# Gathering x rows into the message buffer and scattering 12 of 40 layer-0 groups inside the layer-norm pass of a two-layer graph network

## The chip, the cores and the metric

One core of one Trainium2 chip. The metric is the device time of one execution in microseconds; lower is better. Engines are named TensorE (PE in the rows), VectorE (DVE), ScalarE (ACT), GpSimd (POOL) and SyncE (SP). A name with a q behind it, as SPq, is the engine's sequencer, which issues DMAs.

## What is computed

There are N = 100,000 nodes with 128 features and E = 25,000 edges (`src`, `dst`), sorted by `dst`. `dst` is drawn so that low node numbers are frequent: the edge at share q of the list has a `dst` of about N q squared. `src` is uniform.

```
h  = relu(layernorm(x))                                   # 100,000 x 128
m  = h[src] + relu(edge_attr @ We + be)                   # 25,000 x 128
a  = (1 + eps) * h + segment_sum(m, dst)
a  = relu(batchnorm(a @ W1 + b1)); a = relu(batchnorm(a @ W2 + b2))
x  = x + a
h  = relu(layernorm(x))
deg = count of each node in src;  norm = deg^-1/2[src] * deg^-1/2[dst]
x  = x + segment_sum(norm * h[dst], src) @ W.T + b
```

## The kernel before

The output tensor in HBM serves as `table`: first it holds h, then h plus the aggregated messages, then x of layer 1, then the result. Between stages all engines meet at a barrier (the end of each `nc.Block()`).

**LN pass.** 50 steps over 49 blocks of 2048 nodes and 50 groups of 512 edges. SP loads a block in two halves into one of four buffers, loads the group's edge features, and stores the block of four steps back from one of two output buffers `hb` (L356). VectorE takes statistics of the block (L387) and of the group's gathered x rows (L390), a chain of small operations gives scale `rs` and shift `nm` (L401 to L422), and it makes the messages: `hs` from the gathered rows (L430), then relu plus edge features into `msgs` (L435). ScalarE normalises the block, 16 activations (L467), and may write an `hb` only when the store of two steps back has landed; it also copies TensorE's results (L474, L480). GpSimd gathers the x rows of the group with four indirect DMAs (L373) into a ring of four buffers `xs`; before that it copies the indices to `gi` (L369), and it waits until the messages of four groups back are made. The pass runs in hardware loops with four steps in the body.

**Dedup stage.** An accumulating scatter must not name a row twice in one DMA, and two of them must not overlap on a row. So the messages go out in NS = 40 groups of G1 = 5 tiles of 128 edges. For a group SP loads its keys to all partitions (L650, two buffers), VectorE compares each tile's keys with those of the tiles up to it (`compare`, L740) and works out where each row goes, its own node or a trash row (`place`, L747, L750). TensorE sums equal keys' messages (`sums`, 15 products, L800), ScalarE writes the sums back (L862), and GpSimd scatters the 5 tiles (L701), after the scatter of the group before has landed; it counts landed groups in `s_landed`. In the same loop VectorE writes one-hots of the `src` keys (`one_hots`, L727, L728) and TensorE counts degrees from them (`counts`, L810). There is one set of five one-hot buffers, so `one_hots(g)` waits until TensorE has used those of g - 1. When all are counted the inverse square roots go to a table in HBM (`dis_ready`).

**Pass 1** (matrix W1). SP loads table blocks of 1024 rows (L668), each when enough groups have landed, and TensorE, ScalarE and VectorE transpose, multiply, keep and take statistics. **Pass 2** (W2 statistics) and **pass 3** (W2, add x, store) follow; a third of the intermediate stays in SBUF, in the same memory as `msgs`. **Layer 1's edge part** shares pass 3's block: GpSimd gathers 200 tiles of rows (L1043), each group of them after the blocks it needs are stored and after the SBUF it fills is free, then scatters 25 groups of 8 tiles (L1056) in the way of layer 0.

**Degree gathers.** GpSimd needs 400 small indirect gathers from the degree table (L564). They are spread: from the group after FILL on, EACH of them go ahead of each scatter group; behind the last scatter they go on up to DEG_1, all in the dedup and pass 1 block; pass 2's block takes DEG_1 to DEG_2; pass 3's block takes the rest, ahead of the row gathers. GpSimd's program for a scatter group is

```
if g > FILL:
    if g == FILL + 1: pool.wait_ge(dis_ready, 16 * HALVES)
    gather_degrees(pool, EACH * (g - FILL - 1), EACH * (g - FILL))
pool.wait_ge(s_pay, g + 1); pool.wait_ge(s_dest, g + 1)
if g: pool.wait_ge(s_sent[(g - 1) % 2], ...); pool.sem_inc(s_landed, 1)
```

The dedup stage and pass 1 are one block, in which each engine's program is an unrolled list.

## Time and profile before

| | us |
|---|---|
| median of 3 runs | 2172.61 (2166.89 to 2173.92) |
| the profiled execution | 2184.82 |
| its span | 2183.1 |

| stage | from, to | PE busy | DVE busy | ACT busy | POOL busy | DMA share |
|---|---|---|---|---|---|---|
| LN pass | 14, 424 | 214.8 | 327.5 | 348.6 | 219.7 | 0.85 |
| dedup stage | 427, 672 | 226.3 | 232.1 | 32.8 | 155.6 | 0.43 |
| pass 1 | 672, 1025 | 282.4 | 132.5 | 195.1 | 259.5 | 0.88 |
| pass 2 | 1025, 1237 | 171.5 | 134.7 | 121.8 | 151.3 | 0.52 |
| pass 3 | 1237, 1629 | 293.1 | 186.2 | 225.9 | 284.0 | 0.95 |
| layer 1's edges | 1629, 1729 | 75.5 | 89.3 | 41.6 | 74.2 | 0.36 |
| and its scatters | 1729, 2183 | 213.0 | 205.4 | 106.8 | 322.7 | 0.38 |

Times are from the span's start. Busy is the time in which an engine ran an instruction; waiting and the issuing of DMAs by SP are not in it. GpSimd is busy while it writes the descriptors of an indirect DMA, and the data move afterwards. The DMA share is the mean busy share of the 16 DMA engines. An engine that is busy for much of a stage need not set its length: what does is read from the waits.

### The profile page before, as it was taken

The numbers are of one execution on the slowest core, as the hardware profiler recorded it, in microseconds if no ns is written. First come the engines' busy times: TensorE is split into PE (matmuls) and PEld (weight loads), VectorE is DVE, ScalarE is ACT, GpSimd is POOL, SyncE is SP. The second block draws the span as 40 slices with busy tenths as digits, with TensorE's granted clock in tenths as the row PEclk, the third lists the DMA queues.
The fourth block names the chain that finished last, engine by engine and source line by source line (L and its number), as shares of the span: only waits on it lengthen the run. The fifth ranks groups of instructions, "written<-read, shape, count | busy, mean of one in ns | idle before, by whom it ended". The sixth has DMA issues, their size and how long they took to land. (4 is left out here: it accounts for less than half of the span.)

```text
span 2183.1 us, 27611 instructions
## 1 busy us (share of the span) xinstructions
PE 1478.3 (68%) x7004; PEld 910.7 (42%) x7004; DVE 1312.0 (60%) x4217; ACT 1073.3 (49%) x1794; POOL 1473.3 (67%) x1274
## 2 busy tenths in 40 slices
PE   3555555399996987786999377767767889880000
PEld 1111111177773544443443134434337888880000
DVE  6888888499993433334777245444459999960000
ACT  4999999411114654564776255555543444430000
POOL 5655555066666678875776777677667777677776
PEclk9999999999998999998999699999987999995555
DMA  6999999344437988897665199999992444433333
GB/s 218 316 311 315 316 329 316 98 86 84 86 68 217 342 231 259 254 289 249 216 206 182 47 368 354 359 363 400 394 338 85 85 71 67 69 42 31 31 29 29
DMA packets 213171, 444.70 MB, mean 204 GB/s; under 512 B 64140, under 2 KB 116502, under 8 KB 206826
## 3 DMA queue, kind: packets, MB, share of 16 engines
q1 hardware_dynamic: 128148, 390.58, 49.6%
q0 software_dynamic: 83200, 52.71, 17.4%
q8 instruction: 44, 0.72, 0.1%
q10 hardware_dynamic: 1728, 0.27, 0.1%
q14 instruction: 51, 0.42, 0.1%
HBM read 279.10 MB, written 164.33 MB: 203 GB/s over the span
## 5 line engine op out<-in xcount | busy, mean ns | idle before, releaser
L701 POOL DMA_INDIRECT out_dram<-big,s_dest_ x200 | 322.2, 1611 | 144.7 <-issue 62.5
L1056 POOL DMA_INDIRECT out_dram<-big,t_dest_ x200 | 322.7, 1613 | 130.0 <-DMA out_dram<-big,t_dest_ 70.9
L1219 PE MATMUL psum<-work,w 128*128 128x512 f32 x392 | 204.2, 646 | 135.0 <-ACT work L1168 135.0
L1043 POOL DMA_INDIRECT big<-out_dram,dst_i x200 | 210.3, 1051 | 77.1 <-issue 65.0
L564 POOL DMA_INDIRECT norm<-inv_sqrt_degree,dst_i x200 | 200.9, 1005 | 79.5 <-issue 74.8
L373 POOL DMA_INDIRECT g_x<-in_x_dram,g_i x200 | 190.4, 952 | 88.2 <-issue 47.5
L467 ACT ACTIVATE big<-n_x,n_nm,n_rs 128x128 f32<-128x128 f32 x592 | 231.5, 481 | 25.5 <-DMA out_dram<-big 25.1
L564 POOL DMA_INDIRECT norm<-inv_sqrt_degree,src_i x200 | 191.3, 957 | 71.5 <-issue 59.7
L510 PE MATMUL psum<-WeB,g_eaT 128*128 128x512 f32 x100 | 103.7, 1141 | 168.2 <-ACT g_eaT L474 168.2
L1067 DVE TENSOR_SCALAR work<-work,cols 128x1024 f32<-128x1024 f32 x98 | 74.6, 761 | 236.8 <-ACT work L1176 236.8
L842 PE MATMUL psum<-work,w 128*128 128x512 f32 x392 | 197.0, 628 | 0.0
L522 DVE BATCH_NORM_STATS2 stat<-work 128x6 f32<-128x512 f32 (+1 forms) x138 | 84.9, 659 | 146.3 <-ACT work L858 146.3
L1168 ACT ACTIVATE work<-work,bn_t,bn_s 128x1024 f32<-128x1024 f32 x66 | 81.7, 1240 | 184.0 <-DMA work<-y_feature_major 151.8
L923 PE MATMUL psum<-work,w 128*128 128x512 f32 x392 | 170.9, 599 | 0.0
L818 PE MATMUL psum<-ident,rows 128*128 128x128 f32 x784 | 111.0, 288 | 68.5 <-DMA rows<-out_dram 68.2
L1219 PEld LDWEIGHTS psum<-work,w 128*128 128x128 f32 x392 | 70.8, 201 | 201.1 <-ACT work L1168 119.0
L522 DVE BATCH_NORM_STATS2 stat<-psum 128x512 f32 (+2 forms) x202 | 127.0, 672 | 44.5 <-PE psum L923 44.5
L818 PEld LDWEIGHTS psum<-ident,rows 128*128 128x128 f32 x784 | 94.7, 148 | 134.2 <-DMA rows<-out_dram 89.7
L800 PE MATMUL psum<-big,work 128*128 128x128 f32 x1200 | 144.2, 279 | 6.2 <-DVE work L740 6.1
L800 PEld LDWEIGHTS psum<-big,work 128*128 128x128 f32 x1200 | 139.5, 193 | 17.9 <-DVE work L740 16.1
L862 ACT ACTIVATE big<-psum,sign 128x640 f32<-128x640 f32 x40 | 31.8, 794 | 218.4 <-PE psum L800 218.4
L870 ACT ACTIVATE work<-psum 128x1024 f32<-128x1024 f32 x98 | 100.1, 1021 | 76.5 <-PE psum L818 76.3
(157 smaller groups left out, 3104.3 us busy)
## 6 DMA issues: line engine op xcount, KB each, us to landing
work<-y_feature_major SPq DMA_DIRECT2D x132, 512.0 KB, 6.1
rows<-out_dram SPq DMA_DIRECT2D x98, 512.0 KB, 5.8
rows<-in_x_dram SPq DMA_DIRECT2D x98, 512.0 KB, 6.6
out_dram<-rows SPq DMA_DIRECT2D x97, 512.0 KB, 6.0
out_dram<-big SPq DMA_DIRECT2D x48, 1024.0 KB, 7.5
n_x<-in_x_dram SPq DMA_DIRECT2D x74, 512.0 KB, 5.8
y_feature_major<-work SPq DMA_DIRECT2D x66, 512.0 KB, 5.5
rows<-in_dst_dram SPq DMA_DIRECT2D x39, 320.0 KB, 3.4
```

The costliest lines, as they stand in the source:

```text
L373: pool.indirect_dma_start(out=xs[u][:, j, :], out_offset=None, in_=x[:, :], in_offset=bass.IndirectOffsetOnAxis(ap=gi[u][:, j:j + 1], axis ...
L467: a = act.activation(hb[u % 2][:, c, :], xb[u][:, c, :], ACT.Relu, bias=nm[u][:, c:c + 1], scale=rs[u][:, c:c + 1])
L522: m = dve.bn_stats(kept(stat, n), part)
L564: pool.indirect_dma_start(out=flat(norm[n])[:, t:t + 1], out_offset=None, in_=dis_tab[:, :], in_offset=bass.IndirectOffsetOnAxis(ap=flat(e ...
L701: pool.indirect_dma_start(out=table[:, :], out_offset=bass.IndirectOffsetOnAxis(ap=dest[:, t:t + 1], axis=0), in_=flat(msgs)[:, t * D:(t + ...
L800: m = nc.tensor.matmul(tot_p[g % 2][:, o * D:(o + 1) * D], pairs(g % SAME, j, o, o + 1), flat(msgs)[:, t * D:(t + 1) * D], start=(j == o), ...
L818: m = nc.tensor.transpose(psum[k % 2][:, c * P:(c + 1) * P], rows[k % B][:, c, :], ident[:, :])
L842: m = nc.tensor.matmul(psum[2 + k % 2][:, h * BANK:(h + 1) * BANK], w1[:, :], feats[k % 2][:, h * BANK:(h + 1) * BANK], start=True, stop=True)
L923: m = nc.tensor.matmul(psum[u % 3][:, h * BANK:(h + 1) * BANK], w2[:, :], feats[u % 2][:, h * BANK:(h + 1) * BANK], start=True, stop=True)
L1043: pool.indirect_dma_start(out=msgs[:, g, j * D:(j + 1) * D], out_offset=None, in_=out[:, :], in_offset=bass.IndirectOffsetOnAxis(ap=dst_i[ ...
L1056: pool.indirect_dma_start(out=out[:, :], out_offset=bass.IndirectOffsetOnAxis(ap=dest[:, g * G2 + j:g * G2 + j + 1], axis=0), in_=flat(msg ...
L1219: m = nc.tensor.matmul(psum[u % 2][:, h * BANK:(h + 1) * BANK], w2[:, :], feats[u % 2][:, h * BANK:(h + 1) * BANK], start=True, stop=True)
```

## The change

**Gathers.** GpSimd gathers x rows straight into `msgs`, group after group, with the indices `src_i` itself; `xs`, `gi` and the wait for the messages go. It waits for the gather of two groups back. VectorE reads and overwrites the same tile.

**Twelve groups early.** The LN pass is unrolled. `scatter`, `compare`, `place`, `sums` and `keep` become shared functions. At the steps k = 10, 13, ..., 43 (`early_at`) VectorE compares and places one group behind the messages of that step, TensorE sums it two steps later in `psum[3]` (the edge-feature ring shrinks from four banks to three), and ScalarE keeps it. The key loads stand in SP's queue ahead of a store. GpSimd scatters the twelve groups behind all fifty gather groups, each when the table blocks that it needs have been stored (`n_landed`, `need_0`, worked out by `blocks_needed`).

**The dedup stage** takes groups 12 to 39. The degree counts of all 40 are spread over these 28 (`counted`: one or two each).

**Degree gathers.** FILL 19 to 23, EACH 4 to 5, DEG_1 96 to 170, DEG_2 256 to 330.

The diff, cut to its core (the moved functions are unchanged in what they do):

```diff
-    FILL = 19
-    EACH = 4
-    DEG_1 = 96
-    DEG_2 = 256
+    EARLY, FIRST_AT, SPACING = 12, 10, 3
+    FILL = 23
+    EACH = 5
+    DEG_1 = 170
+    DEG_2 = 330
...
     @block.sync (LN pass)
+        g = early_at(k + 2)
+        if g is not None:
+            wait(sp, s_same, G1 * (g - 1))
+            sp.dma_start(keyT_e[g % 2][:, :], dst[G1 * P * g:G1 * P * (g + 1)].rearrange(
+                "(a e) -> a e", a=1).broadcast_to((P, G1 * P))).then_inc(s_kin[g % 2], 16)
+        if has_block(k - RN):
+            store(k - RN)
...
     @block.gpsimd (LN pass)
-        def gather(i, u):
-            g = RN * i + u
-            wait(pool, g_h, g - RN + 1)
-            pool.sem_inc(pool_go, 1)
-            pool.tensor_copy(gi[u][:, :], kept(src_i, g)).then_inc(g_gi, 1)
-            wait(pool, g_gi, g + 1)
+        for g in range(NG):
+            wait(pool, g_xs[g % 2], 16 * J * (g // 2))
             pool.sem_inc(pool_go, 1)
             for j in range(J):
                 pool.indirect_dma_start(
-                    out=xs[u][:, j, :], out_offset=None, in_=x[:, :],
-                    in_offset=bass.IndirectOffsetOnAxis(ap=gi[u][:, j:j + 1], axis=0)).then_inc(g_xs[u], 16)
+                    out=msgs[:, g, j * D:(j + 1) * D], out_offset=None, in_=x[:, :],
+                    in_offset=bass.IndirectOffsetOnAxis(ap=src_i[:, g, j:j + 1], axis=0)).then_inc(g_xs[g % 2], 16)
+        pool.wait_ge(e_row, 3)
+        for g in range(EARLY):
+            pool.wait_ge(n_landed, pool.value_load(need_0[0:1, g:g + 1], min_val=1, max_val=NBIG))
+            scatter(pool, g)
...
     @block.vector (LN pass)
             messages(k)
+            blocks_needed(k)
+            g = early_at(k)
+            if g is not None:
+                dve.wait_ge(g_msg, k + 1)
+                compare(dve, g, same_e, keyT_e)
+                place(dve, g)
...
     @block.scalar (LN pass)
+            g = early_at(k - 2)
+            if g is not None:
+                keep(act, g, psum[3])
...
     @block.tensor (LN pass)
+            g = early_at(k - 2)
+            if g is not None:
+                sums(pe, g, same_e, psum[3], 1)
...
+            def counted(g):
+
+                done = (g - EARLY) * NS // (NS - EARLY)
+                return range(done, (g + 1 - EARLY) * NS // (NS - EARLY))
...
     @block.vector (dedup stage)
-                    for g in range(NS):
-                        compare(g)
-                        place(g)
-                        one_hots(g)
+                    for g in range(EARLY, NS):
+                        compare(dve, g, same, keyT)
+                        place(dve, g)
+                        for n in counted(g):
+                            one_hots(n)
...
     @block.tensor (dedup stage)
-                    for g in range(NS):
-                        sums(g)
-                        counts(g)
+                    for g in range(EARLY, NS):
+                        sums(pe, g, same, tot_p[g % 2], 2)
+                        for n in counted(g):
+                            counts(n)
```

## Rows read from the trace of the kernel before

**Rows 1.** Stretches: busy us by engine, clock, DMA share, GB/s.

```profile
120.00:200.00 80.00, 43.40 (x51) 12.28 (x50) 68.59 (x343) 73.32 (x198) 46.30 (x53) 1.00 0.93 316
...
1237.00:1629.00 392.00, 293.10 (x1176) 161.13 (x1176) 186.20 (x199) 225.85 (x196) 284.00 (x278) 0.95 0.95 358
```

**Rows 2.** Timeline of ScalarE, LN pass: start, us, instruction, idle before.

```profile
202.30 6.26 ACT L467 ACTIVATE big<-n_x,n_nm,n_rs 128x128 f32<-128x128 f32 x16 [0.94 <-DMA out_dram<-big]
...
209.30 6.25 ACT L467 ACTIVATE big<-big,n_nm,n_rs 128x128 f32<-128x128 f32 x16
...
217.61 6.26 ACT L467 ACTIVATE big<-n_x,n_nm,n_rs 128x128 f32<-128x128 f32 x16 [1.23 <-DMA out_dram<-big]
```

**Rows 3.** Timeline of VectorE and SP in the same steps.

```profile
204.68 0.69 DVE L435 SCALAR_TENSOR_TENSOR big<-g_hs,g_ef 128x512 f32 x1 [0.16 <-DVE g_hs L430]
...
210.12 0.36 SPq L356 DMA_DIRECT2D out_dram<-big  x1
...
211.40 0.69 DVE L435 SCALAR_TENSOR_TENSOR big<-g_hs,g_ef 128x512 f32 x1 [0.16 <-DVE g_hs L430]
```

**Rows 4.** DMA queues and issues of the LN pass, 120 to 360 us.

```profile
q0 software_dynamic: 4016, 8.22, 12.3%
...
g_x<-in_x_dram,g_i POOLq DMA_INDIRECT x126, 4.9
```

**Rows 5.** One group's timeline in the dedup stage; all its compares by line.

```profile
522.47 3.51 PE L800 MATMUL psum<-big,work 128*128 128x128 f32 x30
522.68 0.28 DVE L727 TENSOR_SCALAR rows<-rows 128x256 f16<-128x256 f16 x1
...
524.98 0.34 DVE L740 SCALAR_TENSOR_TENSOR work<-rows,dst_k,upto 128x128 f32<-128x128 int32 x1
...
525.82 2.32 PE L810 MATMUL psum<-rows 128*128 128x512 f16 x10
...
L740 DVE SCALAR_TENSOR_TENSOR work<-rows,dst_k,upto 128x128 f32<-128x128 int32 (+4 forms) x200 | 110.8, 610 | 2.7 <-DMA rows<-in_dst_dram 2.7
```

**Rows 6.** Timeline of SP and GpSimd at both ends of pass 1.

```profile
672.16 4.17 SPq L668 DMA_DIRECT2D rows<-out_dram  x5
...
679.51 1.55 POOL L701 DMA_INDIRECT out_dram<-big,s_dest_  x1 [5.66 <-DMA out_dram<-big,s_dest_]
...
1018.07 0.95 POOL L564 DMA_INDIRECT norm<-inv_sqrt_degree,src_i  x1 [0.30 <-issue]
1025.73 0.94 POOL L564 DMA_INDIRECT norm<-inv_sqrt_degree,src_i  x1 [6.70 <-POOLq L644]
```

**Rows 7.** Groups of GpSimd in pass 1: count, busy, mean ns, idle.

```profile
L701 POOL DMA_INDIRECT out_dram<-big,s_dest_ x106 | 166.6, 1572 | 54.1 <-issue 34.5 <-DMA out_dram<-big,s_dest_ 19.5
L564 POOL DMA_INDIRECT norm<-inv_sqrt_degree,src_i x96 | 92.9, 968 | 33.4 <-issue 28.3 <-DMA out_dram<-big,s_dest_ 5.1
```

**Rows 8.** Groups of GpSimd's instructions, pass 3 to 1729 us.

```profile
L1043 POOL DMA_INDIRECT big<-out_dram,dst_i x200 | 210.3, 1051 | 77.1 <-issue 65.0 <-DMA big<-out_dram,dst_i 10.4 <-ACT work L1168 1.2
L564 POOL DMA_INDIRECT norm<-inv_sqrt_degree,dst_i x144 | 148.0, 1027 | 55.3 <-issue 50.5 <-POOLq L883 4.8
```

**Rows 9.** Timeline, layer 1: first group kept, first scatter.

```profile
1668.12 1.02 ACT L1195 ACTIVATE big<-psum 128x1024 f32<-128x1024 f32 x1 [6.52 <-PE psum L1250]
...
1729.11 2.47 POOL L1056 DMA_INDIRECT out_dram<-big,t_dest_  x1 [5.77 <-issue]
```

**Rows 10.** GpSimd's gathers of x in the LN pass.

```profile
L373 POOL DMA_INDIRECT g_x<-in_x_dram,g_i x200 | 190.4, 952 | 88.2 <-issue 47.5 <-POOL g_i L369 40.7
```

**Rows 11.** DMA queues and issues of pass 1, 690 to 770 us.

```profile
q0 software_dynamic: 4091, 1.58, 18.3%
...
out_dram<-big,s_dest_ POOLq DMA_INDIRECT x25, 6.1
```

**Rows 12.** GpSimd's scatters in the dedup stage.

```profile
L701 POOL DMA_INDIRECT out_dram<-big,s_dest_ x94 | 155.6, 1655 | 90.7 <-DMA out_dram<-big,s_dest_ 35.0 <-issue 27.9 <-ACT big L862 24.3
```

**Rows 13.** SP's loads of pass 1 up to 770 us: first and last start.

```profile
L668 SPq DMA_DIRECT2D rows<-out_dram x36: 327/328/715, 672.2 to 769.0; - x36
```

More of the change, by code:

```diff
@@ new lines, in preln_gin_then_gcn, with scatter @@
+        dest = sb("s_dest_", [P, NTILE], i32, place_scope)
+        NS = NTILE // G1
+        LASTS = E // (P * G1)
+        PAIRS = G1 * (G1 + 1) // 2
+        assert NS * G1 == NTILE and LASTS == NS - 1 and NS <= P and NB <= P and EARLY < LASTS
+        def scatter(pool, g):
+            pool.wait_ge(s_pay, g + 1)
+            pool.wait_ge(s_dest, g + 1)
+            if g:
+                pool.wait_ge(s_sent[(g - 1) % 2], 16 * G1 * ((g - 1) // 2 + 1))
+                pool.sem_inc(s_landed, 1)
+            pool.sem_inc(pool_go, 1)
+            for j in range(G1):
+                t = g * G1 + j
+                pool.indirect_dma_start(
+                    out=table[:, :], out_offset=bass.IndirectOffsetOnAxis(ap=dest[:, t:t + 1], axis=0),
+                    in_=flat(msgs)[:, t * D:(t + 1) * D], in_offset=None, compute_op=ALU.add).then_inc(s_sent[g % 2], 16)
@@ new lines, in compare @@
+        def compare(dve, g, same, keyT):
+            dve.wait_ge(s_kin[g % 2], 16 * (g // 2 + 1))
+            wait(dve, s_tot, g - len(same) + 1)
+            if g == LASTS:
+                dve.memset(keyT[g % 2][:, E - g * G1 * P:G1 * P], PAD).then_inc(s_pad, 1)
+                dve.wait_ge(s_pad, 1)
+            for j in range(G1):
+                t = g * G1 + j
+                dve.scalar_tensor_tensor(out=pairs(same[g % len(same)], j, 0, j + 1), in0=keyT[g % 2][:, 0:(j + 1) * P],
+                                         scalar=flat(dst_k)[:, t:t + 1], in1=upto[:, (G2 - 1 - j) * P:G2 * P],
+                                         op0=ALU.is_equal, op1=ALU.mult, accum_out=seen[:, t:t + 1]).then_inc(s_same, 1)
@@ new lines, in place, with sums @@
+        def place(dve, g):
+            dve.wait_ge(s_same, G1 * (g + 1))
+            dve.scalar_tensor_tensor(out=tiles(hop, g), in0=tiles(seen, g), scalar=1.0, in1=tiles(gap, g),
+                                     op0=ALU.not_equal, op1=ALU.mult).then_inc(s_hop, 1)
+            dve.wait_ge(s_hop, g + 1)
+            dve.tensor_tensor(tiles(dest, g), tiles(hop, g), tiles(flat(dst_k), g), ALU.add).then_inc(s_dest, 1)
+        def sums(pe, g, same, tot, depth):
+            pe.wait_ge(s_same, G1 * (g + 1))
+            wait(pe, s_pay, g - depth + 1)
+            for o in range(G1):
+                for j in range(o, G1):
+                    t = g * G1 + j
+                    m = nc.tensor.matmul(tot[:, o * D:(o + 1) * D], pairs(same[g % len(same)], j, o, o + 1),
+                                         flat(msgs)[:, t * D:(t + 1) * D], start=(j == o), stop=(j == G1 - 1))
+            m.then_inc(s_tot, 1)
@@ L348, in edge_features @@
                                 "(j p) d -> p j d", p=P)).then_inc(g_ea[u], 16)
[L349 removed]
+                            if g == GFULL:
                                 sp.dma_start(ea[u][0:TREST, n, :], edge_attr[TFULL * P:E, :]).then_inc(g_ea[u], 16)
[L352 to L356 removed]
@@ L357, in _, with store @@
-                        steps(sp, NG, RN, load, RN)
+                        def store(k):
+                            sp.wait_ge(n_h, 2 * (k + 1))
+                            lo = SEEN_BIG if k == NBIG - 1 else 0
+                            sp.dma_start(big_rows(table, k, lo), hb[k % 2][lo:P].rearrange("p c d -> p (c d)")).then_inc(n_out[k % RN], 16)
+                        for k in range(NG):
+                            load(k)
                         for k in range(NG - RN, NBIG):
-                            store(k // RN, k % RN)
+                            store(k)
@@ L498, in _ @@
+                        landed(NBIG - 2)
+                        landed(NBIG - 1)
                     @block.tensor
                     def _(pe):
[L500 to L510 removed]
```

348 lines of the change are left out of this document (162 added, 186 removed).

## The prediction

> **What bounds the kernel now.** I read the page's slices first, then the busy time by stage, then inside each stage the timeline around whatever waits. There are six stages: the LN pass (14 to 424 us), the dedup stage of layer 0 (427 to 658, with its degree tail to 672), pass 1 (672 to 1025), pass 2 (1025 to 1237), pass 3 (1237 to 1629), and the edge part of layer 1 with its scatters (1629 to 2183). No engine bounds all of them [rows 1].
>
> The LN pass is held by a loop through two output buffers. An apply that starts at 202.30 takes 6.26 us, its store is issued at 210.12, and the next apply on that buffer starts at 217.61, released by that store: 6.26 + 1.56 + 7.49 = 15.3 us for two steps, 7.65 a step, where ScalarE alone would need 7.0 (202.30 to 209.30) [rows 2, 3]. The store's landing is long because the DMA engines are 0.93 busy [rows 1, 4]. VectorE does a step in 6.7 us (204.68 to 211.40) and finishes a step's messages about 3.5 us before ScalarE ends that step's apply [rows 2, 3].
>
> In the dedup stage TensorE and VectorE share the bound: the group sums take 3.5 us and the group's degree counts 2.3 on TensorE; one-hots 2.3 (522.68 to 524.98) and compares 2.8 (110.8 us over 40 groups), with some 0.4 of placing, on VectorE. 230 us over 40 groups is 5.75 a group [rows 5]. GpSimd scatters meanwhile, and is only at group 19 when the degree table is ready and pass 1 begins to load, at 672.16 [rows 6]. From there GpSimd is the chain: 20 more groups with 4 degree gathers before each, 16 gathers behind them, the last at 1018, and the barrier opens at 1025 [rows 6, 7]. The last blocks of pass 1 wait for the last scatter, so its arithmetic ends no sooner. Pass 2 has 160 degree gathers at 1.25 us, 200 us of its 212. In pass 3 GpSimd does 144 degree gathers and then the 200 row gathers of layer 1, which run 100 us past the end of pass 3; so the layer-1 scatters start at 1729.11, although the first group's sums were kept at 1669.1 [rows 8, 9]. They then run to the end, 18.2 us a group, and ask for nothing but GpSimd.
>
> So what counts is GpSimd's chain from 672 on, and before it the time at which that chain can start.
>
> **The parts of the change, with costs.**
>
> (1) *Gathers straight into the message buffer.* The wait for the messages of four groups back and the small index copy go, and with them 41 us in which the gathers stood behind that copy [rows 10]. GpSimd was not late in the LN pass, so this is worth nothing by itself. It now runs ahead: four gathers at 0.95 + 0.30 are 5.0 us a group, if the group two back has landed. Landing is 4.9 us at present [rows 4, 10]. With the DMA engines fuller I take 5.3, so 50 groups end at 14.5 + 265 = 280 us. Bounds: 5.0 (264) and, with landings of 7 us, 5.75 (302).
>
> (2) *Twelve groups within the LN pass.* VectorE gets 3.3 us more in each third step, 3 x 6.7 + 3.3 = 23.4 us per three steps, 7.8 a step. That is 0.15 above the present 7.65 over the 34 steps between first and last group, 5 us. It starts 3.5 us ahead, so the key load that SP queues before a store finds its buffer free about when SP comes to it. TensorE gets 3.5 us of sums every third step and is busy 43 us of 80, so it has over 3 us free in each; ScalarE gets a copy of 0.8 us every third step and has 0.6 us of waiting in each [rows 1, 2]. Both are covered. The DMA engines get 60 scatters and 12 key loads of 320 KB. A scatter cost about 0.57 us of all 16 engines in pass 1 (18.3% of 80 us for 25 of them, the small gathers between them taken off) [rows 11]; a key load, by its bytes at the LN pass's 316 GB/s, 1.0: 34 + 12 = 46 us, on a pass of 410 us that has some 24 us free at its present share. That makes 20 to 25 us more for the store loop.
>
> GpSimd itself: its scatters can start only after all 50 gather groups, at 280. A group is 5 x (1.66 + 0.30) = 9.8 us, plus the wait for its last landing, 2.4 us when landings take 3.4, and 2.7 more when they take 6.1 as in pass 1 [rows 11, 12]. That is 14.9 a group; 12 groups, less the last wait, 174 us: GpSimd is done at 454 and the barrier opens at 455 or so. Before it opened at 424. So GpSimd ends the LN pass, not the stores (446): **+31 us**. Bounds: landings of 3.4 and gathers at 5.0 put GpSimd at 406, and the stores with half the extra DMA time at 436, +12; gathers at 5.75 and scatters at 16.3 (pass 1's cadence without its gathers) put GpSimd at 490, +66.
>
> The Trainium skill ("SBUF — State Buffer", the box on VectorE blocking DMA) says that GpSimd cannot write its descriptors while VectorE runs an fp32 operation in its two-port mode. The rows show far less: a scatter instruction took 1655 ns while VectorE was busy throughout and 1572 ns in pass 1 [rows 7, 12]. By the rows it is 5 us over 60 scatters, already in the 1.66; by the page, if the 2.8 us of compares of each group stopped GpSimd whole, it would be 34 us more. That is a rival below.
>
> (3) *The dedup stage with 28 groups, but still 40 groups of degree counts.* The counts are spread: 16 groups carry one, 12 carry two. There is one set of one-hot buffers, and a set is rewritten only when TensorE has used the previous one. With two, VectorE writes the first set (2.3), then must wait until TensorE has done the group's sums and the first counts (3.4 + 2.2 after the compares), writes the second (2.3) and only then compares the next group (2.8), for which TensorE waits in turn. So a group with two counts costs 5.5 + 2.3 + 2.8 = 10.6 us and not 5.75 + 2.3 [rows 5]. 16 x 5.75 + 12 x 10.7 = 220 instead of 230, and the tail of 14 us is the same: I take **-8 us**. Bound on the other side: without that stall VectorE's own work sets it, 28 x 6.7 = 188, -42.
>
> (4) *GpSimd around pass 1.* At 12.2 us a group it scatters 12 to 23 within 157 us of the stage's start and then stands before group 24, because the degree gathers wait for the table, some 237 us after the start: 24 groups are done then, before it was 20. From the table on: 16 groups of 5 x (0.97 + 0.30) + 5 x (1.57 + 0.30) = 15.7 us. The landing waits were 19.5 us for 20 groups behind four gathers each, 1 us a group [rows 7]; behind five gathers, 1.25 us more of cover, I take 0.5: 16.2 x 16 = 259. Then 4.5 for the last landing, 90 gathers at 1.25, 112, and 6 of barrier: 382 us. Before, from 672.2 to 1025.1, 353. **+29 us.** Pass 1's own work covers none of it: its loads came at (769.0 - 672.2) / 35 = 2.8 us a block while they had no scatter to wait for [rows 13], which is 98 x 2.8 + 15, about 290 us. Bounds: no landing wait, +21; 0.9 us a group, +36.
>
> (5) *Pass 2* has 160 degree gathers as before: 0.
>
> (6) *Pass 3 and after.* 70 degree gathers instead of 144, at (148.0 + 55.3 - 4.8) / 144 = 1.38 us each [rows 8]: the row gathers start 97 us into the pass, not 199. At 1.44 us [rows 8] they need 288, but the last groups need the last blocks of pass 3 stored, about 400 us into it; they end at 418. The first kept group is there at 432 (1669.1 - 1237). So the scatters start at 432 instead of 492: -60. Against it: some 58 row gathers more fall into pass 3, whose DMA engines are 0.95 busy, at 0.23 us each (12.3% of 240 us for 126) [rows 1, 4], 13 us at most, 8 taken; and three groups more of scatters run beside a busy VectorE, 24 at the 0.1 us above and some landings, 4. **-48 us.** Bounds: -60 and -38.
>
> **Sum** against the profiled execution, 2184.8 us (span 2183.1): 31 - 8 + 0 + 29 - 48 = +4. Its share of the median, 2172.6, is 0.9944; +4 us there is 2177.
>
> **The rivals.**
>
> *The LN pass has room for it* (ends on the other side). Landings stay at 3.4 to 5 us, GpSimd is done at 406 to 420, the stores set the end at 436. For it: the pass is only 0.93 busy, and unrolling spares SP the register arithmetic between its DMAs. Against: pass 1's share of 1.0 brought landings of 6.1. +12 instead of +31: -15 us, 2158. It decides if GpSimd's first scatter group takes under 13 us.
>
> *GpSimd is much later in the LN pass.* Gathers that keep rushing fill the queue, land in 7 us, and the scatters follow at 16.3: +66 instead of +31, +39 in all, 2211. For it: the scatters' rate is pass 1's. Against: the store loop lets the DMA engines rest as soon as it is late.
>
> *The one-hot wait isn't paid,* -42 instead of -8: -30 us, 2143. Against: the buffers are one set in the code, and TensorE's program order is fixed.
>
> *VectorE locks GpSimd out,* 34 us more in the LN pass, +38 in all, 2210. [...] Against: the difference of 0.08 us in [rows 7, 12].
>
> **How the numbers follow.** Forecast 0.43 (its own range, from -13 to +23 us, is 2160 to 2195), room in the LN pass 0.27, GpSimd much later 0.17, no one-hot wait 0.07, lock-out 0.03, something else 0.03. 2177 is the likeliest's time. The range: the bounds and all but the ends of the two outer cases, -32 to +42 us, 2141 to 2214. A measurement of this kernel tells 0.3%, 6.5 us. Of the forecast's 0.43 a fifth is faster than that, two fifths the same, two fifths slower. Faster: 0.09 + 0.22 + 0.07 + 0.01 = 0.39. Same: 0.17 + 0.05 = 0.22. Slower: 0.17 + 0.17 + 0.03 + 0.02 = 0.39.
>
> **What would show it.** LN pass: first scatter near 280 us, one group each 15 us, barrier near 455 with GpSimd last. Dedup stage: 220 us, groups of 5.7 and 10.7 us, TensorE idle some 3 us before the sums that follow a double count. GpSimd idle about 80 us before group 24. Pass 1 about 380 us with GpSimd alone for its last 80 or so. Layer-1 scatters starting right at the first kept group, 432 us after pass 3 starts. The prediction is wrong if the LN pass ends before 440 or after 480, or if the dedup stage takes under 200 us.

## The result, and the profile after

The changed kernel takes 2215.8 us in the median of 4 runs (2206.0 to 2224.7), beside 2173.3 us (2166.9 to 2177.8) for the kernel before on the same chip: ratio 1.019, interval 1.015 to 1.023. It is 43 us slower where +4 was forecast, and 2 us outside the range. The profiled execution has a span of 2223.0 us against 2183.1, so the trace holds 39.9 us of it.

Timeline of the kernel after (start, us, instruction, idle before it and what ended it): GpSimd at the end of the LN pass.

```profile
296.69 0.99 POOL L464 DMA_INDIRECT big<-in_x_dram,src_i  x1 [0.30 <-issue]
297.99 1.62 POOL L183 DMA_INDIRECT out_dram<-big,s_dest_  x1 [0.30 <-issue]
...
314.67 1.97 POOL L183 DMA_INDIRECT out_dram<-big,s_dest_  x1 [7.51 <-DMA out_dram<-big,s_dest_]
...
453.49 1.55 POOL L183 DMA_INDIRECT out_dram<-big,s_dest_  x1 [2.77 <-DMA out_dram<-big,s_dest_]
465.10 1.55 POOL L183 DMA_INDIRECT out_dram<-big,s_dest_  x1 [2.62 <-DMA out_dram<-big,s_dest_]
479.49 0.56 POOL L795 IOTA rows<- 128x512 int32 x1 [5.40 <-POOLq L416]
```

The gathers of x end at 297 us and not at 280. Each L183 row is the start of a scatter group: 17 us apart at first, beside the pass's loads and stores, of which some 7.6 us are the wait for the last landing (16.3 on the average of the seven groups to 412 us), and 11.6 apart at the end, with a wait of 2.7. The barrier opens at 479.5 (before: 424.1). VectorE has nothing to do for the last 58 us, as its row shows. SP issues the last store at 419.9 and waits 18.4 us for it (second row: engine and line, waited for, us in total, times, longest), so the stores are done at some 438.5, and the 41 us from there to the barrier are GpSimd's alone:

```profile
479.50 0.36 DVE L835 TENSOR_REDUCE work<-dst_k 128x40 f32<-128x200 f32 x1 [58.35 <-PEq L416]
...
SPq L416 <- DMA out_dram<-big: 18.4, 1, 18.4
```

The gathers of x and the scatters of the LN pass by group (count, busy us, mean ns, idle before and its causes); below, SP's stores issued from 120 to 297 us (count, KB, us to landing; before, from 120 to 360 us: 7.5), and the stretch 200 to 290 us (busy us by engine, clock, DMA share, GB/s).

```profile
L464 POOL DMA_INDIRECT big<-in_x_dram,src_i x200 | 197.6, 988 | 88.3 <-issue 62.8 <-DMA big<-in_x_dram,src_i 25.5
L183 POOL DMA_INDIRECT out_dram<-big,s_dest_ x60 | 95.1, 1584 | 81.3 <-DMA out_dram<-big,s_dest_ 49.2 <-issue 14.9 <-DVE s_dest_ L224 9.3
...
out_dram<-big SPq DMA_DIRECT2D x22, 1024.0 KB, 8.2
...
200.00:290.00 90.00, 52.42 (x151) 28.62 (x152) 83.74 (x409) 81.59 (x216) 63.85 (x64) 0.62 0.95 326
```

GpSimd stood 25.5 us for landings of its own gathers: (298.0 - 13.6) / 50 is 5.7 us a group, not 5.3.

The dedup stage: a group with two counts and its successor, TensorE's timeline; then two short stretches, in which the granted clock is the third number from the end, behind the five busy times.

```profile
557.73 3.62 PE L233 MATMUL psum<-big,work 128*128 128x128 f32 x30
561.18 2.32 PE L879 MATMUL psum<-rows 128*128 128x512 f16 x10
564.14 2.44 PE L879 MATMUL psum<-rows 128*128 128x512 f16 x10 [0.65 <-DVE rows L833]
568.67 5.24 PE L233 MATMUL psum<-big,work 128*128 128x128 f32 x30 [2.09 <-DVE work L214]
...
570.00:573.80 3.80, 3.80 (x22) 3.79 (x21) 3.80 (x16) 0.00 (x0) 3.19 (x3) 0.55 0.66 104
573.80:576.00 2.20, 2.20 (x12) 1.11 (x11) 0.91 (x4) 0.79 (x1) 1.69 (x2) 1.00 0.55 96
```

The double takes 10.9 us from sums to sums; TensorE stands idle 2.1 us before the next group's sums, and these take 5.24 us instead of 3.51: in the 3.8 us from 570.0 on its granted clock is near the lower of its two levels (0.55; 0.5 is 1.2 GHz, 1.00 is 2.4 GHz). Pass 1 and the rest, GpSimd and SP:

```profile
729.00 0.80 SPq L769 DMA_DIRECT2D inv_sqrt_degree<-rows  x2
732.51 4.04 SPq L783 DMA_DIRECT2D rows<-out_dram  x5
...
993.88 1.55 POOL L183 DMA_INDIRECT out_dram<-big,s_dest_  x1 [0.30 <-issue]
1003.32 1.02 POOL L689 DMA_INDIRECT norm<-inv_sqrt_degree,src_i  x1 [7.88 <-DMA out_dram<-big,s_dest_]
...
1114.91 0.95 POOL L689 DMA_INDIRECT norm<-inv_sqrt_degree,src_i  x1 [0.30 <-issue]
1125.37 0.95 POOL L689 DMA_INDIRECT norm<-inv_sqrt_degree,src_i  x1 [9.52 <-POOLq L759]
...
1334.29 0.95 POOL L689 DMA_INDIRECT norm<-inv_sqrt_degree,dst_i  x1 [4.77 <-POOLq L950]
...
1740.71 0.94 POOL L1108 DMA_INDIRECT big<-out_dram,dst_i  x1 [0.30 <-issue]
1765.87 1.71 POOL L1121 DMA_INDIRECT out_dram<-big,s_dest_  x1 [24.21 <-issue]
...
1763.90 1.03 ACT L1260 ACTIVATE big<-psum 128x1024 f32<-128x1024 f32 x1 [6.60 <-PE psum L1315]
```

They answer to [rows 6, 9]. After the last scatter (993.9) come 110 us of degree gathers and nothing else: in pass 2's first rows ScalarE and VectorE have waited 100 us. The layer-1 scatters now start on the first kept group (1763.90 + 1.03), no longer on the last row gather.

Stage by stage, in us, from the profiled executions. The first load of pass 1 stands for the table.

| Stage | Before | After | Change | Forecast |
|---|---|---|---|---|
| LN pass, to its barrier | 424.1 | 479.5 | +55 | +31 |
| Barrier to the table (dedup stage) | 248.1 | 253.0 | +5 | -8 |
| Pass 1 | 353.6 | 392.9 | +39 | +29 |
| Pass 2 | 211.7 | 208.9 | -3 | 0 |
| Pass 3 to the first layer-1 scatter | 491.6 | 431.6 | -60 | -60 + 8 |
| Layer-1 scatters to the end | 454.0 | 457.1 | +3 | +4 |
| Sum | | | +40 | +4 |

### The profile page after: what moved, and what is told of

Its sections match the earlier page's. It is cut to its first block and busy times, and to the rows that moved or that the text cites. A ratio compares the mean times of both kernels' runs of the same rounds, so it can differ in the third digit from the quotient of the medians.

```text
span 2223.0 us, 26530 instructions
## 1 busy us (share of the span) xinstructions
PE 1458.1 (66%) x7006; PEld 921.0 (41%) x7006; DVE 1313.1 (59%) x4222; ACT 1073.0 (48%) x1794; POOL 1442.2 (65%) x1224
## 5 line engine op out<-in xcount | busy, mean ns | idle before, releaser
L183 POOL DMA_INDIRECT out_dram<-big,s_dest_ x200 | 319.4, 1597 | 175.7 <-DMA out_dram<-big,s_dest_ 90.9
L1121 POOL DMA_INDIRECT out_dram<-big,s_dest_ x200 | 329.6, 1648 | 144.7 <-issue 80.4
L1284 PE MATMUL psum<-work,w 128*128 128x512 f32 x392 | 202.5, 641 | 129.2 <-ACT work L1233 129.1
L1108 POOL DMA_INDIRECT big<-out_dram,dst_i x200 | 204.1, 1021 | 111.5 <-issue 80.4
L464 POOL DMA_INDIRECT big<-in_x_dram,src_i x200 | 197.6, 988 | 88.3 <-issue 62.8
L689 POOL DMA_INDIRECT norm<-inv_sqrt_degree,dst_i x200 | 194.0, 970 | 69.4 <-issue 64.7
L622 PE MATMUL psum<-WeB,g_eaT 128*128 128x512 f32 x100 | 92.3, 1022 | 146.1 <-ACT g_eaT L585 145.9
L912 PE MATMUL psum<-work,w 128*128 128x512 f32 x392 | 186.0, 598 | 0.0
L990 PE MATMUL psum<-work,w 128*128 128x512 f32 x392 | 170.8, 598 | 0.4 <-ACT work L979 0.4
L1233 ACT ACTIVATE work<-work,bn_t,bn_s 128x1024 f32<-128x1024 f32 x66 | 81.7, 1239 | 181.5 <-DMA work<-y_feature_major 152.5
L979 ACT ACTIVATE work<-work,bn_t,bn_s 128x1024 f32<-128x1024 f32 x66 | 81.7, 1240 | 129.2 <-PEq L759 100.2
L233 PE MATMUL psum<-big,work 128*128 128x128 f32 x840 | 112.5, 298 | 29.3 <-DVE work L214 29.3
L887 PE MATMUL psum<-ident,rows 128*128 128x128 f32 x784 | 105.5, 278 | 32.4 <-DMA rows<-out_dram 32.4
L233 PEld LDWEIGHTS psum<-big,work 128*128 128x128 f32 x840 | 109.1, 212 | 38.3 <-DVE work L214 36.9
```

Of the source, the lines that this page charges most:

```text
L183: pool.indirect_dma_start(out=table[:, :], out_offset=bass.IndirectOffsetOnAxis(ap=dest[:, t:t + 1], axis=0), in_=flat(msgs)[:, t * D:(t + ...
L233: m = nc.tensor.matmul(tot[:, o * D:(o + 1) * D], pairs(same[g % len(same)], j, o, o + 1), flat(msgs)[:, t * D:(t + 1) * D], start=(j == o ...
L464: pool.indirect_dma_start(out=msgs[:, g, j * D:(j + 1) * D], out_offset=None, in_=x[:, :], in_offset=bass.IndirectOffsetOnAxis(ap=src_i[:, ...
L689: pool.indirect_dma_start(out=flat(norm[n])[:, t:t + 1], out_offset=None, in_=dis_tab[:, :], in_offset=bass.IndirectOffsetOnAxis(ap=flat(e ...
L887: m = nc.tensor.transpose(psum[k % 2][:, c * P:(c + 1) * P], rows[k % B][:, c, :], ident[:, :])
L912: m = nc.tensor.matmul(psum[2 + k % 2][:, h * BANK:(h + 1) * BANK], w1[:, :], feats[k % 2][:, h * BANK:(h + 1) * BANK], start=True, stop=True)
```

## The experiments

Each is an edit of the changed kernel. The stages are read as above, from GpSimd's timeline of the profiled execution; its time is up to 9 us off the median of its kernel (changed: 2224.7 against 2215.8). The ratio is the measure of a kernel as a whole: beside the experiments the kernel before took 2179 us in the median, and 2173 beside the changed one, so that a difference between the medians of an experiment and of the changed kernel is uncertain by some 6 us. "Dedup and pass 1" runs from the LN barrier to the start of pass 2, and "pass 3" to the first layer-1 scatter. The ratio is to the kernel before. Four kernels with the same LN pass (the changed one, e1, e2, e5) opened that barrier at 479, 474, 472 and 479, so a difference of some 7 us in that stage is not to be explained.

| Kernel | LN | Dedup and pass 1 | Pass 2 | Pass 3 | Rest | Median | Ratio (interval) |
|---|---|---|---|---|---|---|---|
| before | 424 | 602 | 212 | 492 | 454 | 2173.3 | 1 |
| changed | 479 | 646 | 209 | 432 | 457 | 2215.8 | 1.019 (1.015 to 1.023) |
| e1_degrees | 474 | 545 | 211 | 483 | 452 | 2168.1 | 0.995 (0.993 to 0.998) |
| e2_fill31 | 472 | 563 | 209 | 434 | 457 | 2138.4 | 0.983 (0.978 to 0.987) |
| e3_early8 | 433 | 633 | 209 | 431 | 457 | 2166.8 | 0.995 (0.993 to 0.997) |
| e4_mixed | 458 | 636 | 209 | 436 | 451 | 2192.4 | 1.007 (1.005 to 1.009) |
| e5_two_sets | 479 | 600 | 209 | 437 | 457 | 2175.3 | 0.998 (0.995 to 1.000) |
| e6_direct | 428 | 589 | 211 | 487 | 456 | 2173.3 | 0.997 (0.995 to 0.999) |
| e7_all | 439 | 545 | 209 | 439 | 461 | 2092.4 | 0.960 (0.957 to 0.964) |
| e8_mixed22 | 439 | 634 | 209 | 434 | 452 | 2174.4 | 0.999 (0.996 to 1.001) |
| e9_ring3 | 459 | 643 | 209 | 435 | 457 | 2201.5 | 1.010 (1.007 to 1.013) |
| e10_split | 437 | 509 | 196 | 463 | 458 | 2064.0 | 0.948 (0.945 to 0.951) |
| e11_split140 | 437 | 503 | 186 | 480 | 455 | 2066.4 | 0.950 (0.947 to 0.953) |

**e1_degrees: the split of the degree gathers as before.**

```diff
-    DEG_1 = 170
-    DEG_2 = 330
+    DEG_1 = 96
+    DEG_2 = 256
```

> The changed kernel, but with the split of the degree gathers as it was before: 96 of the 400 by the end of pass 1 (not 170) and 160 in pass 2, so 144 in pass 3. Theory A (in pass 1 GpSimd alone sets the time, in pass 3 it does not as long as its row gathers end before the first sums of layer 1 are kept): from the table on GpSimd needs 271 us for its 16 groups, 16 more gathers (20 us) and the 9.5 us at the barrier, 301 us in place of 393, unless the pass's own loads and matmuls need some 290 to 300, which bounds it at about the same figure; so -92 there. In pass 3 the row gathers start 74 gathers later and run past the end of the pass: the layer-1 scatters start 492 us after pass 3's start and not 432, +60. In all -32 us against the changed kernel's 2223 us span, about 2184 in the median. Theory B (pass 1 also waits for something else, its loads or stores beside the scatters, so that fewer gathers do not shorten it): pass 1 stays above 340 us, the end is +10 to +60, over 2225.

Pass 1 fell by 100 us (293 from GpSimd's first degree gather, in place of 393), and the layer-1 scatters came 483 us after the start of pass 3, 51 later than in the changed kernel. The median fell by 48 us. That is theory A's mechanism, with a better price at both ends than it named (-92 and +60). The 74 gathers that were moved forward cost 100 us of pass 1 and buy 51 of pass 3. With 293 us pass 1 is also where the expectation had its loads and matmuls as a bound (290 to 300), so this run does not tell which of the two ends it.

```profile
1706.92 1.71 POOL L1108 DMA_INDIRECT big<-out_dram,dst_i  x1 [0.31 <-issue]
1712.49 1.61 POOL L1121 DMA_INDIRECT out_dram<-big,s_dest_  x1 [3.86 <-issue]
...
1658.35 1.02 ACT L1260 ACTIVATE big<-psum 128x1024 f32<-128x1024 f32 x1 [6.91 <-PE psum L1315]
```

Here the first group was kept at 1659.4, and the scatters waited 53 us for the row gathers, as before the change [rows 9].

**e2_fill31: GpSimd scatters on while the table is not there.**

```diff
-    FILL = 23
+    FILL = 31
```

> The changed kernel, but GpSimd scatters 20 groups (12 to 31) before it waits for the degree table, not 12 (12 to 23), so 8 groups and not 16 are left for pass 1. Theory A (the 94 us in which GpSimd stood before the table were free for scatters): 20 groups at 11.7 us are 234 us, just before the table; pass 1 then has 8 groups of 5 gathers and 5 scatters, 16.2 us each, 130 gathers behind them (163 us) and some 14 us of landing and barrier, 307 us in place of 393; the table comes when it did, 252 us after the barrier. In all -86 us, about 2130 in the median. Theory B (scatters beside the dedup stage hold VectorE or TensorE up, or the loads of pass 1 become the bound at well over 310 us): the stage to the table becomes longer than 258 us, or pass 1 stays over 340 us; -40 or less, over 2175.

Theory A: from the barrier to pass 2 it takes 563 us in place of 646 (-82; -86 expected), and the median fell by 77. SP's first pass-1 load comes 253.2 us after the barrier (725.55 - 472.32), as in the changed kernel, so eight more groups of scatters beside the dedup stage do not delay the table. The rows are this kernel's: the barrier, and the table.

```profile
472.32 0.56 POOL L795 IOTA rows<- 128x512 int32 x1 [5.40 <-POOLq L416]
...
725.55 4.04 SPq L783 DMA_DIRECT2D rows<-out_dram  x5
```

**e3_early8: eight early groups and not twelve.**

```diff
-    EARLY, FIRST_AT, SPACING = 12, 10, 3
+    EARLY, FIRST_AT, SPACING = 8, 10, 3
```

> The changed kernel with 8 groups scattered in the LN pass in place of 12. Theory A (from the end of its gathers, near 297 us, GpSimd alone ends the LN pass, at 17 us a group while the pass's loads and stores run): 8 groups end near 432, the barrier opens between 428 and 436 in place of 479, -43 to -51 us. The dedup stage has 32 groups, 8 of them with a double count; a double costs 11.1 (plus 1.7 at the lower TensorE clock in half of them), a single 5.6: 24 x 5.6 + 8 x 12 = 230, -3. GpSimd has 16 groups before the table (188 us, still done before it), and the rest is the same. In all -45 to -50, about 2168 in the median. Theory B (the stores or VectorE end the LN pass soon after, since the scatters delay them too): the barrier opens over 450, less than -30 us.

```profile
433.04 0.55 POOL L795 IOTA rows<- 128x512 int32 x1 [21.39 <-POOLq L416]
```

The barrier opened at 433, in the range of theory A, with GpSimd waiting 21 us for it: with eight groups GpSimd no longer ends the pass. SP issues its last store there at 415 and waits 17.4 us for it. So the last four groups cost the LN pass 46 us, 11.6 each. In the dedup stage they cost nothing: GpSimd's idle time before the table shrank from 94 to 36 us. The median fell by 49.

**e4_mixed and e8_mixed22: scatters among the gathers.** The two differ in the number (16 or 22); e8 also puts the last two groups behind the last gather.

```diff
-    pool.wait_ge(e_row, 3)
-    for g in range(EARLY):
-        pool.wait_ge(n_landed, ...)
-        scatter(pool, g)
+        e, rest = divmod(g - 16, SPACING)      # in the loop over the gather groups g; e8: 22
+        if rest == 0 and 0 <= e < EARLY:
+            if e == 0:
+                pool.wait_ge(e_row, 3)
+            pool.wait_ge(n_landed, ...)
+            scatter(pool, e)
```

> The changed kernel with the 12 early scatter groups issued among the gathers (one behind every third gather group, from the 17th on) and not behind all of them. Theory A (the cost in the LN pass is GpSimd's order: it stands 7.7 us for each landing with nothing else to issue, after 297 us): the landings are covered by the three gather groups between, GpSimd's work is 50 x 5.3 + 12 x 9.8 = 383 us and it is done before 425; the barrier opens at 425 to 440 in place of 479, -40 to -54 us, about 2168 in the median. The rest is the same. Theory B (the cost is the DMA engines' or the landings' own, whatever the order): scatters among the gathers make the gathers late for VectorE, the steps of the LN pass get longer than 8.3 us and the barrier opens over 460, less than -20 us.

> As the run with the scatters among the gathers, but the first scatter group comes behind the 23rd gather group and not the 17th, and the last two behind the last gather. Theory A (the run before lost its gain because GpSimd stood 40 us for a group's sums to be kept, and so came late with the next gathers, for which VectorE then stood 44 us): with six gather groups more of lead GpSimd waits for no sums and VectorE for no gathers, or under 10 us each; the barrier opens at 430 to 442 us in place of 479 (458 with the smaller lead), -38 to -50 us against the changed kernel, about 2170 in the median. Theory B (scatters among the gathers and the stores lengthen the steps through the DMA engines): the barrier stays over 450.

With 16 it was neither theory: barrier at 458, -21, between the two ranges. GpSimd's scatters in the LN pass, and VectorE's wait for x rows, in e4:

```profile
L183 POOL DMA_INDIRECT out_dram<-big,s_dest_ x65 | 107.7, 1657 | 59.0 <-ACT big L240 39.8 <-issue 18.6 <-DMA big<-in_x_dram,src_i 0.6
...
L486 DVE BATCH_NORM_STATS2 n_st<-big x200: 263/275/296, 20.5 to 429.6; 128x6 f32<-128x128 f32 x100
its engine sat idle before it (us, times) until:
  DMA big<-in_x_dram,src_i: 44.0, 14
```

GpSimd waited 39.8 us for sums to be kept (11.5 of them at the start of the dedup stage) and not once for a scatter's landing; then it came late with the gathers, and VectorE stood 44 us for them. The landings were covered, as theory A says, and VectorE stood for gathers, as theory B says, but for another reason than B's: early group e is placed in step 10 + 3e and summed two steps later, and GpSimd's queue has the wait for these sums ahead of gathers that the next steps need. With six groups more of lead (e8) VectorE waited 5.6 us and the barrier opened at 439, with GpSimd 28 us early for it:

```profile
L489 DVE BATCH_NORM_STATS2 n_st<-big x200: 263/275/295, 20.3 to 403.3; 128x6 f32<-128x128 f32 x100
its engine sat idle before it (us, times) until:
  DMA big<-in_x_dram,src_i: 5.6, 2
...
439.12 0.55 POOL L800 IOTA rows<- 128x512 int32 x1 [28.14 <-POOLq L416]
```

So all twelve groups fit into the LN pass at 11.5 us over a pass with one (428, e6), and 15 over the kernel before. In the changed kernel it was the order, and not the DMA engines, that cost the 40 us more.

**e5_two_sets: a second set of one-hot buffers.**

```diff
-            wait(dve, a_used, G1 * g)
+            wait(dve, a_used, G1 * (g - 1))
 ...
-    dve.tensor_scalar(hot_r[j], ...
+    dve.tensor_scalar(hot_r[g % 2][j], ...      # the same for hot_c and in counts
```

> The changed kernel with two sets of one-hot buffers in the dedup stage, used in turn; nothing else differs. Theory A (a group with two counts is long because the second set has to wait for the first, and the sums after it run at the lower TensorE clock because TensorE stood idle): a double costs VectorE 2.8 + 0.4 + 4.6 = 7.8 us and TensorE 3.5 + 4.4 = 7.9 in place of 11, the sums stay at 3.5 us, so 16 x 5.6 + 12 x 7.9 = 184 us in place of 233; from the barrier to the table 205 us in place of 252.7, GpSimd stands some 47 us before the table in place of 94, and the rest is the same: -45 to -48 us, some 2170 in the median. Theory B (the engines' own work or the landing of the key loads sets these groups): -10 or less.

TensorE's timeline in this kernel, a group with two counts and the sums of the next; then GpSimd's first degree gather:

```profile
571.94 3.51 PE L233 MATMUL psum<-big,work 128*128 128x128 f32 x30
575.29 2.32 PE L879 MATMUL psum<-rows 128*128 128x512 f16 x10
577.45 2.32 PE L879 MATMUL psum<-work 128*128 128x512 f16 x10
579.84 3.62 PE L233 MATMUL psum<-big,work 128*128 128x128 f32 x30
...
...
686.25 1.03 POOL L689 DMA_INDIRECT norm<-inv_sqrt_degree,src_i  x1 [39.31 <-DMA inv_sqrt_degree<-rows]
```

A double takes 7.9 us, as expected to the tenth, the sums behind it 3.6, and GpSimd reaches the table 207.6 us after the barrier (478.7) and not 252.6: -45. The median fell by 41.

**e6_direct: the first part of the change nearly alone.**

```diff
-    EARLY = 12, FILL = 23, EACH = 5, DEG_1 = 170, DEG_2 = 330
+    EARLY =  1, FILL = 19, EACH = 4, DEG_1 =  96, DEG_2 = 256
```

> The first part of the change nearly alone: x rows gathered straight into the message buffer and the LN pass unrolled, but only 1 group scattered early, and the split of the degree gathers and the order of the dedup stage's scatters as before (19 and 4, 96 and 256). Theory A (gathers that run ahead are worth nothing and cost nothing, since the store loop sets the LN pass): barrier at 420 to 430 us, the rest as before, within 6 us of the kernel before, ratio 0.997 to 1.003. Theory B (gathers that rush crowd the DMA engines and the store loop, or SP's and GpSimd's savings shorten it): barrier outside 415 to 435, ratio off by over 0.5%.

Theory A at its edge: ratio 0.997 (0.995 to 0.999), barrier at 427.6. The gathers end at 293 us here too, and behind one scatter group GpSimd stands 125 us. The LN pass is no shorter than before (428 and 424), so gathers that run ahead are worth nothing by themselves. The 13 us less between barrier and pass 2 (589, not 602) go with the one group that was taken out of that stretch: GpSimd comes to its first degree gather 252 us after the barrier and not 265.

**e9_ring3: three groups of x rows in flight and not two.**

```diff
-    g_xs = sems("g_xs", 2)
+    g_xs = sems("g_xs", 3)
 ...
-    wait(pool, g_xs[g % 2], 16 * J * (g // 2))
+    wait(pool, g_xs[g % 3], 16 * J * (g // 3))      # the same in then_inc and in VectorE's wait
```

> The changed kernel, but a group of x rows may be gathered when the group three back has landed, not two back (three semaphores in turn). Theory A (the first scatter came at 298 us and not at 280 because GpSimd stood 25 us for landings of its own gathers, and whatever it saves there comes off the end of the LN pass): gathers at 5.05 us a group end at 266 to 270 us, the scatters follow from there at 15 to 17 us a group, the barrier opens at 450 to 458 us in place of 479, -21 to -29 us. Theory B (the gathers go as fast as the DMA engines take them, or faster ones make the stores and the scatters' landings later by as much): first scatter after 285, or the scatter groups at over 17 us, barrier over 468, -10 us or less.

```profile
274.31 1.96 POOL L183 DMA_INDIRECT out_dram<-big,s_dest_  x1 [0.31 <-issue]
...
459.12 0.55 POOL L795 IOTA rows<- 128x512 int32 x1 [5.56 <-POOLq L416]
```

The scatters start at 274 and not at 298, and the barrier opens at 459 and not at 479: of 24 us, 20 arrive, just short of theory A's range and far from B's. GpSimd waited 4.9 us for landings of gathers and not 25.5. So the two-deep wait of the gathers was a price of the LN pass. The groups are still 15.5 us apart while the pass loads and stores (274.3 to 413.6, nine of them).

**e7_all, e10_split, e11_split140: the repairs together.** All three have e8's order, e5's two sets and `FILL = 28`; they differ in where the degree gathers go:

```diff
-    DEG_1 = 170,  DEG_2 = 330
+    DEG_1 = 150,  DEG_2 = 310      # e7_all
+    DEG_1 = 120,  DEG_2 = 270      # e10_split
+    DEG_1 = 120,  DEG_2 = 260      # e11_split140
```

> All repairs together: scatters of 12 groups among the gathers from the 23rd on, two sets of one-hots, GpSimd scattering to group 28 before the table, 150 degree gathers by the end of pass 1 and 310 by the end of pass 2. Theory A (the four costs found are separate and from the barrier to the end of pass 1 only GpSimd's own work is left): barrier 435; from there 28 groups x 11.9 + 150 x 1.26 + some 20 of start, landing waits and barrier = 540 less what the gathers hide of landings, 525; pass 2 209, pass 3 to the first layer-1 scatter 433, the scatters 456: 2058, some 2060 in the median, ratio to the kernel before 0.944. Theory B (the repairs compete for the same cover, above all pass 1's own loads and matmuls, 290 to 300 us from the table at 205): not under 2100.

> The run with all repairs, with 120 degree gathers by the end of pass 1 (not 150) and 270 by the end of pass 2 (not 310), 130 in pass 3. Theory A (passes 1 and 2 are set by GpSimd's gathers at 1.25 us each, and pass 3 pays for what is left to it only as far as its row gathers run past the first kept sums): pass 1 -37 (under 280 us from its first degree gather, or held at some 270 to 280 by its own loads), pass 2 with 150 gathers -12, the layer-1 scatters 463 us after pass 3's start in place of 439, +24; -25 us against 2092, 2067 in the median. Theory B (pass 2's matmuls set it at 209 whatever the gathers, or pass 1 its loads at over 295): -10 or less, over 2080.

> As the run before in this call, but only 140 gathers in pass 2, so 140 in pass 3. Theory A (pass 2 is GpSimd's alone down to there): pass 2 -25 against 209, 184 us; layer-1 scatters 477 us after pass 3's start, +38; -25 against 2092. Theory B (pass 2 has a floor of its own between 190 and 205 us, from TensorE's 171 us and its loads): pass 2 no shorter than with 150 gathers, so 10 to 14 us slower than the run with 150.

e7 gave 2092: under theory B's 2100, but 32 over the 2060 of A. Most of it is 20 us between barrier and pass 2 (545, not 525). Of GpSimd's 17 groups there before its first degree gather, each took 13 us and not 11.9:

```profile
L183 POOL DMA_INDIRECT out_dram<-big,s_dest_ x85 | 143.8, 1692 | 87.0 <-ACT big L240 36.9 <-issue 25.2 <-DMA out_dram<-big,s_dest_ 24.9
```

GpSimd waits there for sums to be kept too (36.9 us, some 12 of them at the stage's start), and an instruction takes 1692 ns. The repairs are thus not wholly separate. How much of the 13 us is the wait for sums and how much the longer instruction, no run tells. e10 and e11 behave as theory A: pass 2 with 150 gathers takes 196 us and with 140 it takes 186, so it is GpSimd's alone down to there; pass 3 pays 24 and 41 us for what is left to it; 2064 and 2066 in the median, 5% under the kernel before. e10 is the fastest version of this study. Between it and e11 the split is flat. How much of the 5% needs the early groups is not shown: no run has the kernel before with its gathers split and its scatters ordered anew and no group early.

## Why the prediction was wrong

Against the forecast of +4 the trace holds +40. The LN pass, the dedup stage and pass 1 came out 24, 13 and 10 us above their terms, and passes 2 and 3 and the end together 12 us below theirs.

**(1)** *Gathers end at 280* was mis-sized: 297. The step took 5.3 us a group and had 5.75 as a bound; it was 5.7. That a group waits for the landing of the group two back was in the working; the 25.5 us that it would cost were not. e9 priced it: -20 us for a third group in flight.

**(2)** *+31 in the LN pass* is the step that failed most: +55, half a microsecond inside the 480 from which the prediction would have called itself wrong. Its mechanism is right (GpSimd, not the stores, ends the pass), and its size is off at both terms: the start is 18 us late, and from the first scatter to the barrier it takes 479.5 - 298.0 = 181.5 us where 455 - 280 = 175 were forecast. While the pass loads and stores, a group waits some 7.6 us for its landing, where 5.1 were allowed; for the last groups, with the stores done, it is 2.7, which hides most of that error in the sum. What happened is the second rival, "GpSimd much later", at +55 of its +66. "Stores end at 446" was too late: they are done at some 438.5, and e8, where GpSimd stands 28 us early, opens at 439. That is 14 to 15 us over the kernel before and not 22. Whether these are DMA time is open, for VectorE is busy 282 of the 300 us from 100 to 400 (before: 253).

What the forecast did not look for is the order. Behind the gathers GpSimd has nothing else in its queue while a group lands, and each landing costs it the whole wait. e8 gives the same scatters and gathers to the same engine, and takes 40 us less.

**(3)** *-8 in the dedup stage* was mis-sized: +5. The stall itself came as forecast: doubles of 11.0 us on the average of 11 (10.7 forecast). Missing was TensorE's clock. The sums behind six of the 11 stalls took 5.2 us and not 3.5, which made those groups 7.2 us and not 5.65 (9.5 us in all); behind the other five, which stood idle as long (2.1 us), they took at most 3.6, and why is open. The rest are the doubles' own 0.3 us (3 in all) and the stage's first group, 8.6 us where it was 7.3 before. The Trainium skill ("TensorE: Matmul & The Clock Gate", HAM oscillation) describes a TensorE that waits for loads between short bursts, falls back to the lower clock in each wait and starts each burst at it. The trace agrees in kind: 0.55 at 570.0 to 573.8 us behind a TensorE idle for 2.1 us, 1.00 just after, and in e5, without the stall, at most 3.6 us for the sums of every group but the first. e5 shows that stall and clock were worth 45 us together (table at 208 us after the barrier and not 253). Against the kernel before (248) that is -40, where -42 was the bound for a stage without the stall.

**(4)** *+29 in pass 1* was mis-sized: +39. The reading holds in each part: GpSimd stood 94 us before group 24, and then set the pass alone. 16 groups took 263 us (16.5 each, 16.2 forecast), the last landing 7.9 and not 4.5, the 90 gathers 113, the barrier 9.5 and not 6. That 94 idle us could be used here (e2), and that gathers cost more here than they give back (e1), could have been read from the prediction's own numbers (80 us idle; 74 gathers at 1.25 us are 92, for 60 in pass 3), and it did not ask.

**(5)** and **(6)** held: pass 2 -3, the first layer-1 scatter at 431.6 us (432), on the first kept group. Of the +8 for row gathers in pass 3 nothing showed; of the +4 behind, 3 us did.

**The rivals.** *Room in the LN pass*: refuted, its point of decision was a first group under 13 us, and it took 17. *One-hot wait not paid*: refuted in the changed kernel, made true in e5. *VectorE locks GpSimd out*: refuted in size for these compares. A scatter instruction took 1555 ns on the average beside an idle VectorE and 1599 in the LN pass, under 3 us over the 60 early scatters, not 34; the gathers of x, beside which eight of the twelve groups were compared, took 988 ns, and 986 in e6 with one group. It took most in e7's dedup stage, 1736 ns from 450 to 590 us, where VectorE is busy 138.5 of 140 us with compares and one-hots. That is 12% more, and no run shows whether VectorE is the cause. The first row is the changed kernel's from 422 us on, the second its 298 to 421, the third and the stretch e7's 450 to 590.

```profile
L183 POOL DMA_INDIRECT out_dram<-big,s_dest_ x20 | 31.1, 1555 | 21.8 <-DMA out_dram<-big,s_dest_ 16.9 <-issue 4.9
...
L183 POOL DMA_INDIRECT out_dram<-big,s_dest_ x40 | 64.0, 1599 | 59.6 <-DMA out_dram<-big,s_dest_ 32.3 <-issue 10.1 <-DVE s_dest_ L224 9.3
...
L183 POOL DMA_INDIRECT out_dram<-big,s_dest_ x52 | 90.3, 1736 | 58.4 <-ACT big L240 33.1 <-DMA out_dram<-big,s_dest_ 12.8 <-issue 12.5
...
450.00:590.00 140.00, 138.50 (x927) 99.01 (x926) 138.47 (x552) 16.66 (x21) 90.28 (x52) 1.00 0.43 72
```

So the change as a whole: 60 us won in pass 3, given back in three places. The LN pass pays for groups that the dedup stage could have scattered in time that GpSimd then idled; e2 and e3 are two ways to put that right, and each alone beats the kernel before (by 1.7% and 0.5%). Even the 60 us were bought too dear, as e1 shows. What stays open: why a group took 13 us in e7, and the 7 us by which the LN pass differs between kernels in which it is the same.

## What to carry to other kernels

Work moved forward to an engine's idle time is only free if that engine can do it in the order in which its queue has it: put the moved instructions between others that cover their landings, with enough lead that their wait never stands ahead of what the next steps need (e4 and e8 differ in little but that lead, by 19 us). When the balance between two engines changes, read where the freed engine now stands idle, and move the next constants (how many groups before the table, how many gathers in which pass) with it; here the change without this was a loss, and with the order of the queue and a second set of buffers it became a gain of 5%. A stall of TensorE can cost more than its length: behind six of 11 the clock had fallen, and the next sums took 1.6 us longer.

## What the runs showed of the hardware

The recorded clock has to be held against a matmul's own time. In the LN pass before, the record has a granted clock of 1.00 [rows 1], but there two of the pass's matmuls with 512 columns take 2.07 us, just what they take in e6 from 240 to 300 us, where the record says 0.50. In the changed kernel, where it says 0.62, a pair behind a group's sums takes 1.12 us and another 2.07. So by these durations TensorE ran at its lower level in the LN pass before, whatever the record says. The other engines waited 1.0 us for TensorE from 200 to 290 us of the changed kernel, so its clock cost next to nothing there. In the dedup stage record and durations agree (0.55 with 5.24 us, 1.00 with 3.5). The first row is of the kernel before, the next two of e6, the last two of the changed kernel.

```profile
196.42 2.07 PE L508 MATMUL psum<-beB,ones 1*128 1x512 f32 x2
...
242.53 2.07 PE L622 MATMUL psum<-WeB,g_eaT 128*128 128x512 f32 x2 [4.03 <-ACT g_eaT L585]
240.00:300.00 60.00, 32.77 (x39) 9.81 (x40) 51.58 (x253) 52.77 (x143) 43.55 (x42) 0.50 0.97 306
...
221.03 1.12 PE L622 MATMUL psum<-WeB,g_eaT 128*128 128x512 f32 x2
229.25 2.07 PE L622 MATMUL psum<-WeB,g_eaT 128*128 128x512 f32 x2 [5.93 <-ACT g_eaT L585]
```

The landing of a scatter goes with what else the DMA engines do: GpSimd waited some 7.6 us for it beside the LN pass's loads and stores (DMA share 0.94 from 298 to 421 us) and 2.7 us without them (0.29 from 440 to 479), on the same instructions. And GpSimd's scatter instruction took 3 to 12% longer beside a busy VectorE (1599 and 1736 ns against 1555), and was never blocked for long: the longest of those measured above is 2.13 us.
